# One order of SyncE's transfers in two cross attentions, and a clearing of memory moved by one stage

## The reference

```python
qh = q.reshape(b * h, d // h, m)
kh = k.reshape(b * h, d // h, -1)
vh = v.reshape(b * h, c // h, -1)
qk = jnp.einsum('bdm,bdn->bmn', qh, kh) * scale
sm = jax.nn.softmax(qk, axis=-1)
ret = jnp.einsum('bmn,bcn->bcm', sm, vh)
```

## Time and profile before

| | us |
|---|---|
| median of 3 runs (2912.08 to 2914.91) | 2913.16 |
| the profiled execution | 2907.95 |
| its span, first instruction to last | 2906.2 |

### The profile page before, as it was taken

One profiled execution on the slowest core, in us unless ns is written; L12 is line 12 of the kernel. 1 busy time (PEld: TensorE's weight loads), 2 busy tenths in 40 slices (PEclk: granted clock), 3 DMA queues, 4 the chain that ended last, 5 costly groups with the idle time before them and its releaser, 6 DMA issues. The chain is left out here.

```text
span 2906.2 us, 54662 instructions
## 1 busy us (share of the span) xinstructions
PE 2177.5 (75%) x18700; PEld 1525.1 (52%) x18700; DVE 1917.6 (66%) x5805; ACT 1170.6 (40%) x2616; POOL 899.7 (31%) x1488
## 2 busy tenths in 40 slices
PE   3554536888888883399998999388888888639986
PEld 2333324566566652399986777244444444416553
DVE  5999986676777777355555666477677767515345
ACT  1222213555555543122225666155555555313322
POOL 3444442222222222366660000222222222042622
PEclk8766667999999997699999999599999999769998
DMA  3000005443444340300000000544444444022444
GB/s 105 0 0 0 1 3 122 86 91 79 94 79 94 86 85 3 142 2 2 2 2 1 1 2 2 136 88 93 86 95 90 92 86 95 1 82 68 137 135 154
DMA packets 258066, 183.16 MB, mean 63 GB/s; under 512 B 34817, under 2 KB 252065, under 8 KB 257025
## 3 DMA queue, kind: packets, MB, share of 16 engines
q1 hardware_dynamic: 246176, 156.55, 23.8%
q0 software_dynamic: 7456, 18.92, 1.8%
q10 hardware_dynamic: 4160, 4.19, 0.5%
HBM read 94.47 MB, written 83.51 MB: 61 GB/s over the span
## 5 line engine op out<-in xcount | busy, mean ns | idle before, releaser
L750 ACT ACTIVATE xattn_pr<-ps 128x384 f32<-128x384 f32 (+1 forms) x1024 | 537.3, 543 | 449.0 <-PE ps L494 243.3
L478 PE MATMUL ps<-xattn_kp,xattn_qp 96*128 96x192 bf16 (+1 forms) x2048 | 383.1, 270 | 170.5 <-DMA xattn_kp<-xattn_rows 122.1
L624 DVE TENSOR_REDUCE xattn_mx<-ps 128x2 f32<-128x512 f32 x512 | 335.1, 677 | 186.8 <-PE ps L478 182.7
L491 PE MATMUL ps<-xattn_qp,xattn_kp 128*128 128x192 bf16 (+1 forms) x2048 | 419.8, 267 | 8.3 <-DMA xattn_qp<-xattn_mrow 7.7
L620 DVE CUSTOM_DVE_ANT_0 xattn_masked<-ps,xattn_band 128x192 bf16<-128x192 f32 x1024 | 325.3, 354 | 9.8 <-issue 6.3
L509 PE MATMUL ps<-xattn_pr,xattn_vs 128*32 128x256 f32 (+1 forms) x4096 | 313.6, 379 | 12.8 <-ACT xattn_o L755 12.6
L478 PEld LDWEIGHTS ps<-xattn_kp,xattn_qp 96*128 96x128 bf16 x2048 | 183.1, 101 | 237.6 <-DMA xattn_kp<-xattn_rows 115.9
L491 PEld LDWEIGHTS ps<-xattn_qp,xattn_kp 128*128 128x128 bf16 x2048 | 186.8, 99 | 144.4 <-ACT xattn_pr L750 79.4
L494 PE MATMUL ps<-xattn_band,xattn_ident 128*128 128x192 bf16 x1024 | 213.6, 249 | 0.0
L1973 PE MATMUL ps<-rwkv_xm,rwkv_w 128*128 128x256 f32 x384 | 122.0, 492 | 100.9 <-DVE rwkv_xm L2059 100.9
L981 PE MATMUL ps<-ffn_parts,gate_up_t 128*128 128x128 bf16 x3072 | 194.0, 220 | 2.1 <-DVE ffn_parts L1099 2.1
(11 more groups left out here) (305 smaller groups left out, 4460.2 us busy)
## 6 DMA issues: line engine op xcount, KB each, us to landing
xattn_rows<-xattn_parts SPq DMA_DIRECT2D x128, 192.0 KB, 2.1
xattn_qp<-xattn_rows SPq DMA_DIRECT2D x256, 96.0 KB, 3.3
xattn_kp<-xattn_rows SPq DMA_DIRECT2D x256, 96.0 KB, 3.7
xattn_rows<-xattn_parts SPq DMA_DIRECT2D x128, 128.0 KB, 2.1
moe_rows_in<-region_zero SPq DMA_DIRECT2D x6, 1677.0 KB, 7.3
moe_xb<-moe_rows_in SPq DMA_DIRECT2D x78, 129.0 KB, 2.2
xattn_rows<-xattn_parts SPq DMA_DIRECT2D x128, 64.0 KB, 1.8
moe_row<-moe_rows_out SPq DMA_DIRECT2D x16, 512.0 KB, 8.1
```

Of the source, the lines that this page charges most:

```text
L478: mm = nc.tensor.matmul(ps[:, BANK_S + j % RING, mt * D:mt * D + width], qp[u][s][0:R_MAX, h, mt * P:(mt + 1) * P], kp[u][s][0:R_MAX, h, l ...
L491: mm = nc.tensor.matmul(out, kp[u][s][:, h, nt * P:(nt + 1) * P], qp[u][s][:, h, lo:lo + width], start=True, stop=not banded)
L624: ins = nc.vector.tensor_reduce(mx[s][:, h * NT:(h + 1) * NT], ps[:, BANK_S + j % RING, :].rearrange("p (m n) -> p m n", m=NT), AX.X, ALU.max)
L750: nc.scalar.activation(out, src, ACT.Exp, scale=HD ** -0.5).then_inc(exped, 1)
```

## The change

In the cross attentions SyncE's list has `place(p + 2, u, 0)` directly behind the stores and ahead of `place_maxima(p + 1, 1 - u, 0)`. `place` waits for the transposed scores of the heads that last read its tile for s = 0 too (before, that wait followed from the maxima ahead of it). The three transfers of a row of maxima become one, whose destination has three partitions and whose source has 48. The waits for it count 16 where they counted 48. `clear_regions` is called at the start of the causal attention's stage, not ahead of the gated MLP; it stays a block of its own, and its tile lives for that stage.

```diff
                 def place(p, u, s):
                     if s == 0:
-
                         sp.wait_ge(stored[u], by_parity(p, u, 96))
-                    else:
-                        wait(sp, scores_t, idx(p - 2, HW * (s + 1)))
+                    wait(sp, scores_t, idx(p - 2, HW * (s + 1)))
                     for m, to in enumerate((qp, kp)):
...
                 def place_maxima(p, u, s):
                     sp.wait_ge(max_kept, run(p, s) + 1)
-                    for part in range(PARTS):
-                        row = qp[u][s][R_MAX + part:R_MAX + part + 1, :, :].rearrange("a h (m n) -> a (h m) n", n=P)
-                        sp.dma_start(row, mrow[s][part * MX:(part + 1) * MX, :]).then_inc(rows_in[u][s], 16)
+                    rows = qp[u][s][R_MAX:R_MAX + PARTS, :, :].rearrange("r h (m n) -> r (h m) n", n=P)
+                    sp.dma_start(rows, mrow[s][:]).then_inc(rows_in[u][s], 16)

                 def step(p, u, first, last):
...
                     if there(p + 2):
                         store(p + 2, u)
+                        place(p + 2, u, 0)
                     if not last:
                         place_maxima(p + 1, 1 - u, 0)
                     if there(p + 2):
-                        place(p + 2, u, 0)
                         place(p + 2, u, 1)
...
-                        pe.wait_ge(rows_in[u][s], by_parity(p, u, 48))
+                        pe.wait_ge(rows_in[u][s], by_parity(p, u, 16))
...
-                        a.wait_ge(rows_in[1 - u][s], by_parity(p - 1, 1 - u, 48))
+                        a.wait_ge(rows_in[1 - u][s], by_parity(p - 1, 1 - u, 16))
...
             gu, pj = ternary_weights(core, own, rows, landed)
-            regions, cleared = clear_regions(core, own)
             gated_mlp(core, "ffn0", FF // 256, ...)
+        core.end_stage()
+
+        with ExitStack() as stage:
+            regions, cleared = clear_regions(core, stage)
+            causal_attention(core, "attn1", attn, b_q, b_k, b_v, b_o)
             nc.sync.wait_ge(*cleared)
-        core.end_stage()
-
-        causal_attention(core, "attn1", attn, b_q, b_k, b_v, b_o)
         core.end_stage()
```

## The result

| | kernel before | changed kernel |
|---|---|---|
| median, 5 runs each | 2913.16 us (2909.58 to 2914.91) | 2943.84 us (2934.65 to 2949.78) |
| span of the profiled execution | 2906.2 us | 2941.7 us |

The ratio is 1.0101 (95% interval 1.0078 to 1.0123): the change costs 30.7 us, where 35 were forecast. In the code of after the lines from 440 on stand three lower: 552 is now 549, 491 is 488, 478 is 475, 836 is 833, 440 is 437; 434 is 432.

The account below looks back on a forecast made before the run. TensorE is busiest in both cross attentions, in a step loop through stores, place and scores. xattn0 +54, xattn1 -24, start -2, regions 0, clock +7 give +35 us on 2913.16: 2948 us, 8-in-10 range 2908 to 2985.

Parts of the forecast that it names:

- The place moves forward: Both cross attentions, SyncE: the place is issued once the stores land, 0.6 us earlier in xattn0, 2.3 in xattn1.
- What is queued behind it: SyncE's queue: maxima behind four places land only with them, 4.9 us after the first place's issue; alone 1.7 us.
- Who waits, xattn0: TensorE at j = 14 waits 2.5 us for maxima; chain delays line 552; step 22.2 against 20.43, +1.8 us.
- rival 2: xattn0: chain through VectorE and GpSimd doesn't bind; +0.6 us a step, 2905 us; 0.13 for cases between it and forecast.
- Who waits, xattn1: TensorE waits 1.1 us for maxima, but the chain behind is shorter; step 18.6 against 19.38, -0.8 us.
- The merged transfer: Maxima on SyncE: saves two issues of 0.6 us, on the path only at each stage's start; -2 us in all.
- The landing on fewer engines: Merged transfer's landing: 0.2 us earlier than taken (near end, chosen) to 0.75 later (far end, +45 us over 60 steps).
- The regions: Clearing moved ahead of the causal attention: still a block, 24 us in the open either way; effect 0.
- rival 1: Both cross attentions: maxima don't queue behind places, landing 1.9 us after issue; -41 us, 2872 us; chance 0.12.
- rival 3: Both cross attentions: TensorE's wait for the places is simply removed; up to -100 us, 2813 us; chance 0.02.
- rival 4: The clearing overlaps with the causal attention: -24 us on top, 2924 us; chance 0.04.
- rival 5: Worse than forecast: merged transfer at its far end, or half clock in most xattn0 steps; above 2965 us; chance 0.12.

## Why the prediction was right, and where it was not

The sum came out at +35 us and +30.7 was measured. The mechanism of the loss is shown. But one edit was judged wrongly, and a gain was put down to another. That the sum came so near is in part luck: on the profiled executions the change costs 35.5 us, of which xattn1's steps give 8 us more than forecast (-31.1 over 29 steps, where -0.8 a step makes -23) while the starts cost about 10 more (+7.8 against -2), and the two cancel.

- **The place moves forward**: right. SyncE issues it when the stores have landed (12.45 us into the step of xattn0, 9.77 in xattn1), and the wait ahead of the first scores is gone. In means over 29 steps that is 1.2 us earlier than before (13.64) in xattn0 and 2.8 (12.61) in xattn1, where one step of each had given 0.6 and 2.3.
- **What is queued behind it**: right, and it is the core. 4.9 us from the first place's issue to the landing were forecast; the matmul runs 5.1 us after it. That what is queued does it is shown by the maxima behind none, two and four places at the same wait for the stores: 15.32, 15.83 and 17.50 us to the matmul of j = 14, and 2855, 2851 and 2944 us in all. The wait alone costs 10 us.
- **Who waits, xattn0**: right in its place, nearly right in size. 22.2 us were forecast (22.4 with the clock), 22.42 measured. The new wait is 2.1 us a step where 2.5 were worked out. The chain through VectorE and GpSimd binds, and is worth 0.9 us a step where 1.2 were forecast; rival 2 (it doesn't bind) put the step at 21.0, and with the chain relieved it was 21.5. The wait of line 549 for GpSimd, forecast at about 1.2 us a step, grew from 14.4 to 22.8 us, 0.3 a step; another 0.3 shows up ahead of line 475, which waits for the maxima of heads (20.1 us where it was 12.3). The size of that wait was wrong, though the step was right.
- **Who waits, xattn1**: the number held (-0.8 forecast, -1.1 measured), the reason did not. The prediction took the gain for one of the place that moves. Merging alone gives -1.75 a step there, and the order then takes 0.6 back. The order alone gives -0.63: with three issues ahead of the place it gains, with one ahead of it it loses.
- **The merged transfer** is the step that failed: "In mid stage they lie beside other work", and -2 us in all. That looked only at when the maxima land. It left out who stands behind them on SyncE: the places, for which TensorE waited 1.6 and 1.8 us a step. Merging is worth 67 us by itself, and on top of the new order 1.0182 - 1.0101 of 2913, 24 us. The sum came out right all the same, since its other terms were read for the new order as a whole: the place at the landing of the stores, where nothing issues ahead of it, and the maxima 4.9 us behind its first issue. A part of the merge's gain lies in them, under the name of the move.
- **The landing on fewer engines**: as far as the consumer shows it, the near end was right. (The far end, 0.75 us a place, works out at 0.72 from the numbers given for it.) The Trainium skill ("DMA: Bandwidth & Descriptors", section "Why a DMA increments its semaphore by 16 and not by 1") says that only the engines a transfer uses write to its semaphore, and that their number divides the slowest dimension of both sides. The traces agree. The DMA queue q1 with its packets, MB and share of 16 engines' span, first of the kernel before:

```profile
q1 hardware_dynamic: 246176, 156.55, 23.8%
```

Of the version with two transfers:

```profile
q1 hardware_dynamic: 242336, 156.53, 24.2%
```

And of the changed kernel:

```profile
q1 hardware_dynamic: 240416, 156.52, 20.2%
```

By that rule a row costs 48 writes in three transfers, 2 + 16 in two and 3 in one. Over 128 rows that is 3840 and 5760 fewer, and the packets fall by 246176 - 242336 = 3840 and 246176 - 240416 = 5760. Behind places, three engines instead of 16 make the row hardly later: its consumer runs 5.1 us behind the first place, where the near end was 4.9 for the landing. How long the merged row takes by itself no trace shows.
- **The regions**: right, 24 us in the open in either place (ratio 1.0005).
- **The starts** were forecast at -2 us and went the other way, by 2.8 and 5.0 us; the longest new wait, 6.0 us, is in xattn1 ahead of the steps counted here. There it is the order: from the stage's first transfer to the first of the matmuls counted it takes 58.5 to 60.4 us in the four versions with four places ahead of the maxima, and 54.9 to 56.4 in the five with the row right behind the stores' issue. In xattn0 it stays open: its start also differs by 1.7 us between the kernel before and the one that moves only the clearing.
- **The clock**: it fell as forecast, 0.99 to 0.94 in xattn0. Its price there (7 us were put in) can be bounded. Up to j = 14 a step of the changed kernel takes 17.50 - 2.14 = 15.36 us without the new wait, and the version that only merges, at 0.99, takes 15.35; from j = 14 to the next line 549 it is 4.92 against 4.78. So it is an estimated 4 us at most over 29 steps. TensorE's slower work falls largely into time in which the step waits anyway.

Rivals 1, 3, 4 and 5 fell: the maxima do queue, a new wait took the place of the old, the clearing overlaps with nothing, and 2943.84 us is below 2965. Rival 2 fell too, but the chain was worth less than forecast.

## What to carry to other kernels

Where engines wait for large transfers, count what their queue issues ahead of them: leaving out two small issues of 0.5 us each gave 67 us here, more than any order of the same transfers gave. A small transfer on the path goes ahead of large ones, or behind as few as its slack covers (in xattn0 two places cost 0.4 us a step and four cost 2.3; in xattn1 two cost nothing and brought the step down by 0.4). When a wait goes and the loop doesn't get faster, as in xattn0, look for the chain that was second, here one vector instruction placed between two maxima, and relieve it as well; work out the cost of every edit of a change alone as well as together, or two errors can make a right sum.

## What the hardware did that I had not expected

- Issuing goes by the number of transfers far more than by their size: one from 48 partitions to three takes 0.73 us, one of the three from 16 to one 0.59 in the median, and a row in two transfers takes 1.24 us, in three 1.77. An issue by ScalarE takes the same 0.73 us, and here ScalarE had less room for it than SyncE.
- With the maxima behind four places the places themselves land sooner (medians of 2.9 us for q and 3.2 for k, against 3.3 and 3.8 in the version that only merges), and the share of the DMA engines in xattn0 is 0.32 in the changed kernel and 0.43 there, for the same bytes a step. What the engines' time goes to there is not shown.
